# Second attention of a fused block: spacing of the value packs, place of the row-sum groups, and how the row sums are inverted

## The reference

```python
q, k, v = (...)                                   # (4, 8 heads, 2048, 32)
attn = jnp.einsum('bhqd,bhkd->bhqk', q, k) * scale
attn = jax.nn.softmax(attn, axis=-1)              # exp(attn - row maximum) / row sum
attn_out = jnp.einsum('bhqk,bhkd->bhqd', attn, v)
```

## Time and profile before

| | |
|---|---|
| median of three runs | 6836.81 us |
| profiled execution, its own time | 6836.09 us |
| its span, first to last instruction | 6834.3 us |
| mean granted TensorE clock over the span | 0.904 |
| busy share: TensorE matmul, VectorE, ACT, GpSimd | 87%, 78%, 59%, 32% |
| second attention, first to last turn of the maxima | 4804.2 to 6603.4 us |

### The profile page before, as it was taken

How to read it: one execution, slowest core, us unless ns; L and a number is a source line. 1 busy time by engine, 2 the same in 40 slices (tenths; PEclk the granted TensorE clock), 3 DMA queues, 4 the chain that set the end, 5 groups by cost and what they waited for, 6 DMA issues and landing times. The chain is left out here.

```text
span 6834.3 us, 116275 instructions
## 1 busy us (share of the span) xinstructions
PE 5932.6 (87%) x39184; PEld 2657.6 (39%) x39184; DVE 5352.9 (78%) x7287; ACT 4013.1 (59%) x7095; POOL 2186.3 (32%) x1050
## 2 busy tenths in 40 slices
PE   5996766775999999999999999765999999999993
PEld 3443541442333333333333333333444444444432
DVE  6996510775999998998999999587878788878855
ACT  3773101111888888888888888611466666656660
POOL 2331100342000000000000000011788888888891
PEclk9998866776999999999999999865899999999995
DMA  3113576445233333233233333177111111111106
GB/s 139 50 46 100 171 257 221 137 162 135 43 48 52 53 52 47 45 53 47 45 53 52 48 48 48 40 241 206 35 38 38 38 38 34 34 35 38 38 6 200
DMA packets 373238, 548.75 MB, mean 80 GB/s; under 512 B 68464, under 2 KB 273200, under 8 KB 352976
## 3 DMA queue, kind: packets, MB, share of 16 engines
q1 hardware_dynamic: 359888, 524.77, 31.8%
q10 hardware_dynamic: 12800, 16.78, 0.7%
HBM read 352.02 MB, written 186.78 MB: 79 GB/s over the span
## 5 line engine op out<-in xcount | busy, mean ns | idle before, releaser
L671 DVE TENSOR_REDUCE at_NM<-at_MX 128x1 f32<-128x1024 f32 (+1 forms) x4096 | 3732.7, 951 | 594.4 <-PE at_MX L508 566.3
L617 ACT ACTIVATE at_PB<-at_S 128x512 f32<-128x512 f32 x6144 | 3314.5, 599 | 1049.6 <-PE at_S L537 956.2
L508 PE MATMUL at_MX<-at_KT,at_QT 48*128 48x512 f32 (+1 forms) x6144 | 2400.8, 457 | 162.9 <-DVE at_NM L671 84.3
L537 PE MATMUL at_S<-at_QT,at_KT 50*128 50x512 f32 (+1 forms) x6144 | 2369.2, 437 | 6.7 <-ACT at_PB L617 3.7
L548 PE MATMUL at_AV<-at_PB,at_VS 128*32 128x256 f32 (+1 forms) x20480 | 1839.5, 441 | 18.4 <-ACT at_AVS L625 13.2
L537 PEld LDWEIGHTS at_S<-at_QT,at_KT 50*128 50x128 f32 (+1 forms) x6144 | 1024.1, 189 | 930.7 <-issue 506.6
L508 PEld LDWEIGHTS at_MX<-at_KT,at_QT 48*128 48x128 f32 (+1 forms) x6144 | 990.0, 191 | 745.2 <-DVE at_NM L671 550.5
L474 POOL TENSOR_TENSOR at_SUM<-at_SUM,at_PB 128x2048 f32<-128x2048 f32 x192 | 888.4, 4627 | 64.5 <-ACT at_PB L617 47.9
L456 POOL CAST at_NMR<-at_NMF 16x128 fp32r<-16x128 f32 x96 | 26.8, 280 | 2705.7 <-ACT at_NMF L630 2705.7
L548 PEld LDWEIGHTS at_AV<-at_PB,at_VS 128*32 128x32 f32 x20480 | 433.0, 109 | 1027.5 <-ACT at_PB L617 732.2
L474 POOL TENSOR_TENSOR at_SUM<-at_PB 128x2048 f32<-128x2048 f32 x160 | 749.5, 4685 | 145.1 <-ACT at_PB L617 144.3
(11 more groups left out here) (153 smaller groups left out, 4106.0 us busy)
## 6 DMA issues: line engine op xcount, KB each, us to landing
moe_W<-in_w SPq DMA_DIRECT2D x64, 1024.0 KB, 10.8
at_QT<-qk SPq DMA_DIRECT2D x384, 128.0 KB, 5.5
at_KT<-qk SPq DMA_DIRECT2D x384, 128.0 KB, 6.6
qk<-r_HI SPq DMA_DIRECT2D x64, 512.0 KB, 3.6
qk<-r_LO SPq DMA_DIRECT2D x64, 512.0 KB, 4.4
x<-r_X SPq DMA_DIRECT2D x48, 512.0 KB, 3.0
at_VS<-v SPq DMA_DIRECT2D x96, 256.0 KB, 8.4
at_QT<-qk SPq DMA_DIRECT2D x96, 256.0 KB, 4.1
```

The lines of the kernel that those rows point to most:

```text
L508: ins = nc.tensor.matmul(MX[r][:, a, :], QT[u][h:h + NQ, b * P:(b + 1) * P], KT[u][h:h + NQ, (c + a) * W:(c + a + 1) * W], start=True, sto ...
L537: nc.tensor.matmul(SP_[item(it, s, "score", t)[1]][:, :], KT[u][h:h + NQ + 2, kb * P:(kb + 1) * P], QT[u][h:h + NQ + 2, c * W:(c + 1) * W] ...
L617: nc.scalar.activation(PB[:, t % NPB, :], SP_[r][:, :], ACT.Exp, scale=scale).then_inc(exp_done, 1)
L671: nc.vector.tensor_reduce(NM4[:, b, c:c + 1], MX[r][:, :, :].rearrange("p a n -> p (a n)"), AX_X, ALU.max, negate=True).then_inc(ring_got, 1)
```

## The change

Four edits, all in `phase_attention`, and all without effect on the first attention.

1. `value_step` loses its `v | 1`: each key block has its own step, 6, 10, 14, ... 66.
2. `sum_step` becomes the step of the value pack two blocks later. `outputs` issues value packs first, so a row-sum group stands directly behind a value pack: steps 30, 46, 54, 70 and 78.
3. The row sums are inverted on ACT: `put_sums` takes the logarithm of `L`, waits for it, and takes the exponential of its negative into `REC`. VectorE's four reciprocals are gone. At the stage's start ACT is given a table set that holds both functions.
4. The multiplication by the inverse stands at step 84 (step 20 of the next window) instead of 88.

```diff
     def value_step(v):
-        return NCH * (v if TWO else v | 1) + NCH - 1 + LAG
+        return NCH * v + NCH - 1 + LAG
...
     def sum_step(i):
-        return NCH * GROUPS[i][1] + LAG + 10
+        return value_step(GROUPS[i][1] + 2)
...
-            def put_sums(it):
-
-                wait(act, rec_done, NCH * it)
+            def put_sums(it, s):
+
+                wait(act, rec_done, it)
                 wait(act, l_done, len(GROUPS) * (it + 1))
-                nc.scalar.activation(LS[:, :], L[:, :], ACT.Copy).then_inc(ls_ready, 1)
+                nc.scalar.activation(LS[:, :], L[:, :], ACT.Ln).then_inc(ls_ready, 1)
+                wait(act, ls_ready, it + 1)
+                wait(act, norm_done, it - 1)
+                nc.scalar.activation(REC[s % 2][:, :], LS[:, :], ACT.Exp, scale=-1.0).then_inc(rec_done, 1)
...
+            if not TWO:
+                nc.scalar.preload_act_table_set("natural_log_exp_and_others")
             take_turned(0, 0, 0)
...
-            def invert(it, s, q):
-
-                if q == 0:
-                    wait(dve, norm_done, it - 1)
-                    wait(dve, ls_ready, it + 1)
-                part = slice(q * W // NCH, (q + 1) * W // NCH)
-                nc.vector.reciprocal(REC[s % 2][:, part], LS[:, part]).then_inc(rec_done, 1)
-
             def normalise(it, s):
-                wait(dve, rec_done, NCH * (it + 1))
+                wait(dve, rec_done, it + 1)
...
             def outputs(n, s, t):
-                for q in range(NCH):
-                    if sum_step(len(GROUPS) - 1) + 3 + 2 * q == t:
-                        invert(n, s, q)
-                if sum_step(len(GROUPS) - 1) + 3 + 2 * NCH == t:
+                if sum_step(len(GROUPS) - 1) + 6 == t:
                     normalise(n, s)
```

More of the change, by code:

```diff
@@ L649, in window @@
                         if not TWO and sum_step(len(GROUPS) - 1) + 1 == t_:
-                            put_sums(it)
+                            put_sums(it, s_)
                     if TWO and t == OUT_STEP and (not isinstance(n, int) or n > 0):
@@ L660, in _ @@
             else:
-                put_sums(N - 1)
+                put_sums(N - 1, N - 1)
         @block.vector
```

## The result

| | before | after |
|---|---|---|
| median on one chip, 15 runs each | 6827.36 us (6819.48 to 6839.26) | 6841.84 us (6834.71 to 6863.38) |
| profiled execution | 6836.09 us | 6854.94 us |
| period of a unit, mean of thirty | 58.12 us | 58.72 us |
| normalisation in the middle of the stage | 3.89 us | 4.49 us |

The ratio is 1.0025, with a 95% interval of 1.0017 to 1.0033: the change makes the kernel slower by a quarter of a per cent. The prediction said 6827 us, that is 9 us faster. The time lies in its range, the sign is wrong. The ratios in this document compare executions that lie within 1.5% of the fastest of their kernel; where executions lie further off, they are listed one by one.

The account below looks back on a forecast made before the run. The order of work between TensorE and VectorE, neither alone, was taken as the bound. A unit of 53.3 + 3.6 + 1.0 = 57.9 us against 58.12, and 2.8 us off the stage's end, gave 6827 us, range 6785 to 6960.

Parts of the forecast that it names:

- TensorE's own work, 53.3 us: Per unit of the second attention: 30.1 us of steps plus 23.2 of packs, single ones 1.18, doubles 2.04.
- The 0.8 us between the packs and the 2.35 us at the reciprocals go: TensorE's waits in undisturbed stretches and around the row-sum copy and reciprocals vanish from each unit.
- ACT's chain costs nothing: Logarithm and exponential take 1.3 us against the copy's 0.59, hidden by the packs; without cover 0.7 us more.
- Normalisation of 4.4 us, a pause of 3.1 to 3.2, a wait of 3.6: At step 20 VectorE waits out GpSimd's third addition; TensorE stands 3.2 us and loses 3.6 in all per unit.
- The clock falls in nearly each unit: Behind the new pause of about 3.1 us at the normalisation, TensorE's granted clock drops to 0.50.
- Its price, 1.0 us: Cost per unit of the slow clock behind the pause, chosen between bounds of 0 and 1.65 us.
- End of the stage, 1.3 us: From the inversion to the last normalisation 1.3 us instead of 4.12, a saving of 2.8 us.
- the bound of 3.3/2 us: Upper limit, 1.65 us a unit, on the price of one slow-clock stretch of some 3.3 us.
- 1 (the clock stays up): The clock behind the pause doesn't fall or its fall is hidden: period 56.9 us, total 6797 us; chance 0.24.
- 2 (VectorE passed over): At the third addition's end GpSimd keeps the port; normalisation waits 4.65 us more per unit, total 6967 us; chance 0.17.
- 3 (no addition met): GpSimd runs over 0.8 us later, so the normalisation slips in ahead: period 53.3 + 0.5, total 6705 us; chance 0.06.
- 4 (ACT): Table loads at each change, or TensorE waiting for the exponentials: 22 or 82 us more, 6849 or 6909; chance 0.11.

Follow-up runs that it names:

- rec_psum: The changed kernel with ACT's exponential written over the row sums in PSUM, so the normalisation reads one SBUF and one PSUM tile: 6692.56 us, ratio 0.9795.
- act_only: The kernel before with only the inversion moved to ACT, value packs in pairs and normalisation at step 24 as before: 6875.45 us, ratio 1.0054.
- pairs_psum: The kernel before with the inversion on ACT and the inverse in PSUM, value packs still in pairs, normalisation at step 24: 6715.10 us, ratio 0.9838.
- hold2: The changed kernel with the inverse in PSUM, plus two unread VectorE reciprocals before the normalisation (2.17 us, all but 0.85 lost): 6717.26 us, ratio 0.9834.
- norm82: The changed kernel with the normalisation two steps earlier, at step 18 of the next window instead of 20: 6707.93 us, ratio 0.9814.
- before_psum: The kernel before with VectorE's reciprocals written into the PSUM bank of the row sums, which the normalisation then reads: 6779.60 us, ratio 0.9926.

## Why the prediction was wrong

Own steps, each with what it measured:

- *TensorE's own work, 53.3 us.* Right: 53.32 in rec_psum. Single packs cost what the row-sum group cost; a second pack directly behind takes 0.88.
- *The 0.8 us between the packs and the 2.35 us at the reciprocals go.* Right: packs 3.05 us apart outside the pause, one wait of TensorE's matmuls for VectorE left in a unit.
- *ACT's chain costs nothing.* Right for the changed kernel, where the packs stand every four steps. The cover is real: with pairs (act_only, pairs_psum) the same chain costs 1.0 us (4.56 against 3.54).
- *Normalisation of 4.4 us, a pause of 3.1 to 3.2, a wait of 3.6.* Right: 4.49, 3.09, and 3.64 by the rule of hold2.
- *The clock falls in nearly each unit.* Right: in all thirty.
- *Its price, 1.0 us.* **This is the step that failed.** It was 58.72 - 53.32 - 3.64 = 1.76 us.
- *End of the stage, 1.3 us.* Right: 1.29.

So every mechanism was forecast and one term was mis-sized, by 0.76 us. Thirty times that is 23 us, and the whole miss is 24: forecast 9 us less, measured 15 more. The price had two parts. The usual fall, as in 24 of the units, costs 1.34 us: their periods lie between 58.17 and 58.61 (the last one is 57.35), with a mean of 58.30, against 53.32 + 3.64 = 56.96. The 1.4 us that one slow stretch costs in act_only, read there without the rule of hold2, agree. I had subtracted too much for what the pause and VectorE's slower pace cover. Once the normalisation is done, VectorE takes 0.61 us for a maximum, but TensorE needs 0.86 for a step at 1.2 GHz (5546.28 to 5547.14 in the unit shown), so it is TensorE that sets the pace at once. And in six units a second slow stretch follows the first, as in the windows above, which the bound of 3.3/2 us didn't provide for: four periods of 59.7 to 59.8 and two of 61.65, together (4 x 1.45 + 2 x 3.35)/30 = 0.42 us in the mean. Such a stretch begins with VectorE and ACT partly idle and covers nothing. What decides whether it comes isn't shown.

The price could have been read from the kernel before. In its thirty units the clock fell 19 times. Thirteen of the falls lay under the normalisation and cost nothing (periods of 57.7 to 57.8 us, as without a fall). The six others lay bare behind the normalisation: five slow stretches of 3.4 us cost 1.4 us each (periods of 59.1 to 59.3), and one of 10.2 us cost 4.7 (62.46). The windows view has a bare one and a hidden one in two units that follow each other:

```profile
5382.79:5442.06 59.27, 56.04 (x301) 26.42 (x298) 46.82 (x70) 35.11 (x67) 51.85 (x14) 0.97 0.15 36
5442.06:5499.83 57.77, 56.23 (x301) 26.09 (x297) 46.75 (x70) 35.20 (x67) 51.62 (x14) 0.97 0.16 38
```

The thirty units had 71.7 us at 0.50 before and 129.7 after. The error was to choose a middle of the two bounds, when the argument beside it ("the second is bare") already said which kind the new falls would be, and the periods said what that kind costs.

The rivals: 1 (the clock stays up) didn't occur; it did in hold2, with a pause of 0.76 us. 2 (VectorE passed over) didn't occur in the changed kernel but is real four steps on, at 6 us a normalisation, which the sum of it, 4.65 us dearer, had right. 3 (no addition met) is what norm82 comes near to, 54.09 forecast as 53.8. 4 (ACT) didn't occur with these packs. The 0.29 for slower held mostly the large cases; with the clock's price open up to its own bound, more of the forecast's 0.42 belonged there: at 1.65 instead of 1.0 the sum alone is 10 us slower than before.

The larger miss is of another kind. The prediction explained the 4.4 us well and took them as given. Moving one operand to PSUM removes the wait in them, and then the same change saves 2.05%.

## What to carry to other kernels

When a VectorE instruction lasts several times its own duration beside a GpSimd one, move one of its inputs out of SBUF before tuning the order around it: with both inputs in SBUF each part of the change cost time by itself, with one in PSUM each saved some. A stall of TensorE is priced with the clock that follows it (here 3.6 us of waiting and 1.8 of slow clock), and a slow stretch of 3.4 us cost 1.3 to 1.7 us wherever TensorE's own work set the pace, and nothing under a wait. Don't place an instruction on the edge of another engine's where both sides wait: the time then differed by up to 3% from execution to execution of one program.

## What the runs showed of the hardware

- A pause of about 3.1 us in an otherwise dense stream brought TensorE down to 1.2 GHz in thirty of thirty units; one of 0.76 us (hold2, pairs_psum) never did. But the length of one pause doesn't decide it: behind the same pause of 2.7 us the clock fell in 27 units of act_only and stayed up in 3, and in before_psum it fell in 16 of thirty units whose longest pauses were 0.7 us, two of them 2 us apart at the reciprocals. In the changed kernel the slow stretch lasted 3.4 us in 24 units, 6.8 in four and 10.2 in two, with TensorE busy again.
- Two engines that both wait for the shared port are served in no fixed order: 1.46 or 6.07 us for the same instruction in the same place, and executions of 6690 or 6901 us for the same kernel.
- Logarithm and exponential of 512 columns start 0.63 us apart on ACT, with a wait for the result between them (5537.11, 5537.74), so the hand-over costs some 0.04 us.
